# Vision tower on one core: the pre stage of the local attention moved into its loop, keys and values unpadded

## What is computed

```
h = window_attention(x)                        # 8x8 windows, rotary, 8 heads of 8
h = h + local_attention(layernorm(h))          # the part that changes
h = h + routed_ffn(layernorm(h))
h = h + decayed_linear_attention(layernorm(h))
h = h + binary_gated_ffn(layernorm(h))
```

## Time and profile before

| | us |
|---|---|
| median of 3 runs | 1968.52 (1965.01 to 1970.42) |
| the profiled execution | 1966.1 |
| its span, first to last instruction | 1964.3 |
| busy: TensorE, weight loads, VectorE, ScalarE, GpSimd | 1667.3, 1223.0, 1181.7, 975.4, 422.3 |
| mean granted clock of TensorE | 0.959 |

### The profile page before, as it was taken

One profiled execution on the slowest core, in us unless ns is written; L12 is line 12 of the kernel. 1 busy time (PEld: TensorE's weight loads), 2 busy tenths in 40 slices (PEclk: granted clock), 3 DMA queues, 4 the chain that ended last, 5 costly groups with the idle time before them and its releaser, 6 DMA issues.

```text
span 1964.3 us, 94305 instructions
## 1 busy us (share of the span) xinstructions
PE 1667.3 (85%) x35690; PEld 1223.0 (62%) x35690; DVE 1181.7 (60%) x3445; ACT 975.4 (50%) x1765; POOL 422.3 (21%) x477
## 2 busy tenths in 40 slices
PE   5999999856568888888888779999999999999996
PEld 3566666644356666667667556666666666666663
DVE  2466656577534444444444467777777777777772
ACT  2344444423322222222222227777777777777776
POOL 2100000034323232333323222222222222222210
PEclk8899999988889999999999869999999999999998
DMA  4000000135533333333333213333333333333332
GB/s 127 16 11 13 11 11 13 32 64 102 99 94 92 96 92 96 91 96 93 95 96 93 65 29 81 79 80 79 79 80 80 80 80 80 80 80 80 80 79 57
DMA packets 254173, 141.71 MB, mean 72 GB/s; under 512 B 181314, under 2 KB 218050, under 8 KB 253858
## 3 DMA queue, kind: packets, MB, share of 16 engines
q1 hardware_dynamic: 254114, 140.88, 29.8%
HBM read 63.56 MB, written 18.42 MB: 42 GB/s over the span
## 4 chain that ended last, share of the span: by engine, by line
PE 37%; issue 30%; SPq 24%; DVE 5%; DMA 1%; POOL 1%; ACT 1%; DVEq 0%; POOLq 0%; ACTq 0%
SPq L402 12%; PE ps_D L805 11%; DVE prob L1304 4%; SPq L391 3%; PE ps_AV L822 3%; SPq L373 2%; PE ps_J L913 2%; PE ps_J L881 2%; PE ps_J L863 2%; PE ps_OT L891 1%; PE ps_J L939 1%; PE ps_OT L931 1%; PE ps_D L923 1%; PE ps_OT L956 1%; PE ps_OT L875 1%
## 5 line engine op out<-in xcount | busy, mean ns | idle before, releaser
L1062 ACT ACTIVATE prob<-ps_D 128x1024 bf16<-128x1024 f32 x448 | 450.5, 1022 | 80.9 <-PE ps_D L805 80.6
L1234 DVE TENSOR_REDUCE m_sb<-ps_D 128x4 f32<-128x400 f32 x256 | 135.4, 571 | 204.5 <-PE ps_D L708 188.9
L1050 ACT ACTIVATE prob<-ps_D 100x512 f32<-100x512 f32 x256 | 138.8, 594 | 216.9 <-PE ps_D L730 216.9
L493 POOL TENSOR_TENSOR tile_a<-q_st,q_mask 128x1024 f32<-128x1024 f32 x64 | 123.3, 1926 | 404.2 <-DMA q_st<-q_d 346.9
L730 PE MATMUL ps_D<-tile_a,key_patch 64*100 64x128 f32 x2048 | 176.7, 288 | 0.0
L726 PE MATMUL ps_D<-mT,key_rows 64*100 64x128 bf16 x1024 | 129.4, 224 | 50.8 <-ACT mT L1039 32.2
L1187 DVE TENSOR_REDUCE top<-ps_D 128x8 f32<-128x512 f32 x128 | 79.5, 684 | 148.0 <-PE ps_D L582 148.0
L805 PE MATMUL ps_D<-tile_b,w_parts 128*128 128x256 bf16 x1024 | 154.2, 273 | 15.7 <-DVE prob L1304 8.3
L805 PE MATMUL ps_D<-tile_a,w_parts 128*128 128x256 bf16 x1024 | 155.6, 275 | 13.8 <-DVE prob L1304 7.2
L730 PEld LDWEIGHTS ps_D<-tile_a,key_patch 64*100 64x100 f32 x2048 | 146.9, 166 | 0.0
L1304 DVE TENSOR_SCALAR prob<-ps_D 128x1024 bf16<-128x1024 f32 x64 | 78.4, 1225 | 77.9 <-PE ps_D L805 77.9
(11 more groups left out here) (174 smaller groups left out, 3874.9 us busy)
## 6 DMA issues: line engine op xcount, KB each, us to landing
tile_b<-v_d SPq DMA_DIRECT2D x640, 40.0 KB
tile_a<-xg SPq DMA_DIRECT2D x384, 64.0 KB, 2.0
tile_b<-xg SPq DMA_DIRECT2D x384, 64.0 KB, 2.0
key_st<-k_d SPq DMA_DIRECT2D x64, 175.0 KB, 3.0
key_st<-k_d SPq DMA_DIRECT2D x64, 167.0 KB, 3.1
w_exp<-experts SPq DMA_DIRECT2D x64, 129.0 KB, 2.3
k_d<-kpad SPq DMA_DIRECT2D x32, 140.0 KB, 2.3
xin<-in_x SPq DMA_DIRECT2D x32, 128.0 KB, 2.2
```

The costliest lines, as they stand in the source:

```text
L493: gp.tensor_tensor(q_block[:, par, :].rearrange("c (p h q) -> c p h q", h=NH, q=NQ), q_st[:, :].rearrange("c (p a q) -> c p a q", a=1, q=N ...
L1050: act.activation(prob1[0:NKL, 2 * g + x, :], s_loc[x][0:NKL, :], ACT.Exp).then_inc(T2["exp_done"], 1)
L1062: act.activation(sgn[:, k % 4, :], unit(k, par)[:, :], ACT.Sign).then_inc(BN["sign"], 1)
L1234: dve.tensor_reduce(m_sb[:, C * x + HOT[x] + 4 * g:C * x + HOT[x] + 4 * g + 4], m_loc[x][:, 0:4 * NKL].rearrange("p (u n) -> p u n", u=4), ...
```

## The change

Pre and local become one loop over strips of 256 tokens. Each engine's `front` first does the pre work of 5 strips (`LEAD`), then strip i of the loop also does the pre work of strip i+5. On VectorE and GpSimd the moments, 1/std and normalised rows are one strip further ahead (`made`). The order on TensorE within a strip is new: both `peak` halves come right after the `scores` halves, the maxima are transposed ahead of the second `values`. The pre products use free columns of the banks T, OT and J1.

In DRAM the tokens lie unpadded, all images one after the other, with a guard at both ends. Within a row the 64 columns are ordered by column modulo 4 (four groups of 16), so ScalarE writes `xnp` in this order. The ten key columns of the 16 patches are then three groups (4, 3 and 3 columns), each of which is a run of 16 neighbouring tokens, so the values come in three transfers of 4 KB pieces, which ScalarE issues. GpSimd makes `key_patch` with two copies instead of one. Keys outside an image are no longer zeros but what lies there; the edge flags mask them as before. SyncE stores a strip's keys, queries and values in one transfer each. `strips_ahead` writes out two strips ahead of the loop and six behind it.

```diff
-PW = W + 2 * HALF
+NC = W // QP
+GUARD = 16
+EDGES = GUARD + HALF * W
+FLAT = B * H * W + 2 * EDGES
...
-        kpad, q_sb, v_sb = sb("kpad", [C, 2, WIN * PW]), sb("q_sb", [P, 2, 512]), sb("v_sb", [P, 2, 4, C])
+        xn = sb("xn", [P, 2, C])
+        xnp = sb("xnp", [P, 2, 256])
...
         xfgT, xrT = sb("xfgT", [P, 256]), sb("xrT", [P, 256])
         ln_sb = {}
...
+            full = (NSTRIP - LEAD - 1) // 2
+            with eng.Fori(1, full) as j:
                 strip(j, 0)
                 strip(j, 1)
-            strip(NSTRIP // 2 - 1, 0)
...
+                strip(j, 0)
+                strip(j, 1)
+
+        def ahead(j, par):
+
+            i = j * 2 + par
+            m = i + LEAD
+            return m if not isinstance(i, int) or m < NSTRIP else None
+
+        def made(j, par):
+
+            i = j * 2 + par
+            return min(i + LEAD + 1, NSTRIP) if isinstance(i, int) else i + LEAD + 1
...
+        def value_rows(i, group):
+
+            first, n = ((0, QP), (1, 3), (NC - 1, 3))[group]
+            src = v_d[bass.ds(i * (QP * W) + GUARD + first, NC), :]
+            return bass.AP(src.tensor, src.offset, [[W * C, KS], [NC * C, n], [1, NC * C]])
+
+        def value_keys(par, group):
+
+            at, n = ((0, QP), (QP * KS, 3), (7 * KS, 3))[group]
+            return v_patch[at:at + KS * n, par, :, :].rearrange("k a c -> k (a c)")
 
...
+            def store_rows(m, par):
+                at = bass.ds(m * (QP * W) + EDGES, QP * W)
+                sp.wait_ge(L["k_sb"], times(m + 1))
                 settle(sp)
...
+                sp.dma_start(k_d[:, at], kpad[:, par, :]).then_inc(L["stored%d" % par], 16)
+                sp.wait_ge(L["q_sb"], times(m + 1))
                 settle(sp)
...
+                sp.dma_start(q_d[bass.ds(m, 1), :, :].rearrange("t (x c) n -> c (t x) n", c=C),
                              q_sb[C:P, par, :].rearrange("c (a n) -> c a n", n=P)).then_inc(L["stored%d" % par], 16)
-                sp.wait_ge(L["v_sb"], times(i + 1))
+                sp.wait_ge(L["v_sb"], times(m + 1))
...
+                sp.dma_start(v_d[at, :].rearrange("(p t) c -> p (t c)", t=2), v_sb[:, par, :, :].rearrange("p t c -> p (t c)")).then_inc(L["stored%d" % par], 16)
+
+            def stored(pair, par):
+                sp.wait_ge(L["stored%d" % par], times((pair + 1) * 48))
+
+            def keys_in(i):
+                sp.wait_ge(T2["k_patch"], times(i * 2))
                 settle(sp)
                 for x in range(2):
-                    n = KS * PW - 32 * x
...
+                    sp.dma_start(key_st[rows_of(x), :], k_d[:, bass.ds(i * (QP * W) + GUARD - 8 + 8 * x, KS * W + 8)]).then_inc(T2["k_in"], 16)
                 sp.wait_ge(T2["q_block"], times(i))
                 settle(sp)
                 sp.dma_start(q_st[:, :], q_d[bass.ds(i, 1), :, :].rearrange("a r n -> (a r) n")).then_inc(T2["q_in"], 16)
+
+            def edge_in(i, par):
                 sp.wait_ge(T2["scores"], credited((i - 1) * 2))
...
-                sp.dma_start(key_rows[EDGE[0]:C + EDGE[1] + 1, par, :], a["edge"][bass.ds(s, 1), :, :].rearrange("a x n -> (a x) n")).then_inc(T2["edge_in%d" % par], 16)
...
-                    src = v_d[bass.ds(b, 1), bass.ds((s * QP + r) * PW, PW), :].rearrange("a n c -> (a n) c")
-                    sp.dma_start(v_patch[r * KS:(r + 1) * KS, par, :, :], bass.AP(src.tensor, src.offset, [[C, KS], [QP * C, 16], [1, C]])).then_inc(T2["v_in%d" % par], 16)
-
...
-                    strip_in(b, pair * 2, 0)
-                    strip_in(b, pair * 2 + 1, 1)
...
+            def front():
+                store_rows(0, 0)
+                store_rows(1, 1)
+                sp.wait_ge(L["padded"], times(16 * 4))
+                stored(0, 0)
+                stored(0, 1)
+                keys_in(0)
+                store_rows(2, 0)
+
+            def strip(j, par):
+                i = j * 2 + par
+                flat = isinstance(i, int)
+                edge_in(i, par)
+                if not flat or i + 2 < NS:
+                    stored(j + 1, par)
+                if not flat or i + 1 < NS:
+                    keys_in(i + 1)
+                if not flat or i + 3 < NS:
+                    store_rows(i + 3, 1 - par)
+
+            strips_ahead(sp, front, strip)
...
                 v = buf[:, :]
-                return bass.AP(v.tensor, v.offset, [list(v.ap[0]), [QP, 8], [PW, KS], [1, KS]])
+                near = bass.AP(v.tensor, v.offset + 8, [list(v.ap[0]), [1, 8], [NC, QP * KS]])
+                far = bass.AP(v.tensor, v.offset + 9, [list(v.ap[0]), [1, 8], [NC - 2, 2], [W, KS], [NC, 3]])
+                return near, far
...
+            def norm_and_bias(m):
+                inv_std("pre", L, m)
+                bias_rows(m)
+
+            def bias_rows(m):
+                gp.wait_ge(L["xn"], times((m + 1) * 2))
                 settle(gp)
...
+                gp.tensor_tensor(h[:, bass.ds(m * 2, 2), :], h[:, bass.ds(m * 2, 2), :],
+                                 bias2[:, :].rearrange("p (a c) -> p a c", a=1).broadcast_to((P, 2, C)), ALU.add).then_inc(L["biased"], 1)
...
+                keys = key_patch[:, par, :].rearrange("c (p n) -> c p n", p=8)
+                near, far = patches(key_st)
+                gp.tensor_copy(keys[:, :, 0:QP * KS], near).then_inc(T2["k_patch"], 1)
+                gp.tensor_copy(keys[:, :, QP * KS:NKL].rearrange("c p (b r w) -> c p b r w", b=2, r=KS), far).then_inc(T2["k_patch"], 1)
...
+            def front():
+                for m in range(LEAD + 1):
+                    norm_and_bias(m)
+                gp.wait_ge(T1["scores"], times(NT * 2))
+                strip_patches(0, 0)
+                strip_patches(1, 1)
+
+            def strip(j, par):
+                i = j * 2 + par
+                m = made(j, par)
+                nxt = not isinstance(i, int) or i + 2 < NS
+                if not isinstance(m, int) or m < NS:
+                    inv_std("pre", L, m)
+                if nxt:
+                    strip_patches(i + 2, par)
+                if not isinstance(m, int) or m < NS:
+                    bias_rows(m)
+
+            strips_ahead(gp, front, strip)
...
+            def pre_values(m, par):
+                pe.wait_ge(L["xT_sb"], times(m + 1))
+                pe.wait_ge(L["v_sb"], times(m))
                 settle(pe)
-                for t in range(4):
-                    mm = pe.matmul(bank["J2"][:, t * C:(t + 1) * C], xnp[:, par, t * P:(t + 1) * P], w_v2[:, :], start=True, stop=True)
+                for t in range(2):
...
                 mm.then_inc(L["v_ps"], 1)
 
...
+            def pre_keys(m, par, added):
+                pe.wait_ge(L["k_sb"], times(m))
+                pe.wait_ge(L["q_sb"], times(m))
+                pe.wait_ge(T2["h_done"], times(added))
+                settle(pe)
+                pe.matmul(bank["J1"][:, 256:512], w_kq2[:, :], xnp[:, par, :], start=True, stop=True).then_inc(L["kq_ps"], 1)
...
             def strip(j, par):
                 i = j * 2 + par
+                m = ahead(j, par)
                 first, last = isinstance(i, int) and i == 0, isinstance(i, int) and i == NS - 1
                 scores(j, par, 0)
+                if not last:
+                    peak(*after(j, par), 0)
+                if m is not None:
+                    pre_turn(m)
                 if not first:
-                    project(i - 1)
+                    project(i - 1, min(i + LEAD, NS) if isinstance(i, int) else i + LEAD)
+                if m is not None:
+                    pre_values(m, 1 - par)
                 scores(j, par, 1)
                 if not last:
-                    peak(*after(j, par), 0)
+                    peak(*after(j, par), 1)
                 values(j, par, 0)
+                if m is not None:
+                    pre_keys(m, 1 - par, i)
                 if not last:
-                    peak(*after(j, par), 1)
+                    turn_maxima(i + 1, made(j, par))
                 values(j, par, 1)
-                if not last:
-                    turn_maxima(i + 1)
 
             strips_ahead(pe, front, strip)
-            project(NS - 1)
...
+            def pre_turned(m, par):
+                act.wait_ge(L["xT_ps"], times(m + 1))
+                act.wait_ge(L["kq_ps"], times(m - 1))
+                act.activation(xnp[0:C, par, :].rearrange("c (r b q) -> c r b q", r=QP, b=QP),
+                               bank["T"][0:C, 256:512].rearrange("c (r q b) -> c r b q", r=QP, b=QP), ACT.Copy).then_inc(L["xT_sb"], 1)
+
...
+            def values_in(i, par, group):
+                act.wait_ge(T2["av_done"], credited((i - 1) * 2))
+                settle(act)
+                act.dma_start(value_keys(par, group), value_rows(i, group)).then_inc(T2["v_in%d" % par], 16)
 
             def strip(j, par):
                 i = j * 2 + par
-                for g in range(2):
+                m = ahead(j, par)
+                more = not isinstance(i, int) or i + 1 < NS
+
```

(37 more changed lines are left out.)

186 lines of the change are left out of this document (73 added, 113 removed).

## The result

The changed kernel takes 1852.44 us (median of 4 runs, 1851.32 to 1856.05) beside 1966.76 of the kernel before in the same comparison (1961.82 to 1970.42): a ratio of 0.942, 95% interval 0.940 to 0.945, **faster**. The profiled execution took 1851.3 us, 1849.4 of it in the span; 1851.8 had been forecast for it.

A forecast was written before the change was run, and what follows sets the result against it. SyncE's issues were taken to set the 8.80 us strip. First scores at 427.5 plus 576.2 of loop (58 strips at 9.03) end the local stage at 1003.7, not 1118: 114.3 less, 1854 us, range 1840 to 1881 (0.62).

The forecast's parts named there:

- its sum of 5.95 us: SyncE per strip: 8.80 less 5.55 for ten value issues, plus 2.7 for three stores, under the strip's 9.03.
- The front: Pre work of five strips ahead of the loop: 2.8 us a turn, first scores at 427.5, bounds 422 and 436.
- Rival E: Front: six GpSimd power-and-bias pairs and the first stores hold it to 460; +33 us, 1887; chance 0.06.
- TensorE's own work: TensorE in a strip: 7.51 us, the stretch less two waits, kept unchanged, plus 1.32 of pre work.
- The projection's margin: TensorE's cover while VectorE makes the weighted outputs: thin, 0.3 us; 0.20 a strip left for such waits.
- the step on **VectorE: VectorE in a strip: 4.1 us busy plus 1.5 of pre work, 5.6 of 9.03.
- GpSimd's copies: Two strided key_patch copies: 1.1 us a strip, bounds 0.87 and 2.6; margin 1.6 us at 0.87.
- Rival B: GpSimd late with the patches, deciding once copies exceed 2.5 us; at 3.6, +64 us, 1918; chance 0.05.
- rival C: SyncE's store wait joins stores and loads into one ring of 13.1 us a strip; +236 us, 2090; chance 0.02.
- A: Hand-over waits stay at 1.19 us a strip, a fifth piece on every engine pushing others; +57, 1911; chance 0.14.
- F: Moving issues to ScalarE frees nothing, both engines' issues sharing one place; 11.5 us a strip, +143, 1997; chance 0.01.
- D: Loop: all waits gone and added work 1.1, a strip of 8.6 us; 1829; chance 0.10.

The follow-up runs named there:

- experiment 1: Changed kernel, with SyncE instead of ScalarE issuing the three value transfers, in the same strip, not one ahead: 1859.71 us, ratio 0.944.
- experiment 2: Changed kernel, with SyncE issuing the values in ten transfers a strip instead of three by ScalarE: 2139.39 us, ratio 1.086.
- pre apart (3): Changed kernel, with all 64 turns of pre work ahead of the first strip and none in the loop: 2033.16 us, ratio 1.033.
- experiment 4: Changed kernel, with all pre work ahead of the loop and SyncE issuing the queries before the keys: 1942.01 us, ratio 0.985.
- experiment 11: Changed kernel, with the old order of peaks and their transpose on TensorE and of maxima on VectorE: 1890.08 us, ratio 0.961.
- gap and queries first (9): Changed kernel, with the normalise between the two maxima and SyncE loading queries ahead of keys: 1812.74 us, ratio 0.9205.
- experiment 6: Changed kernel, with the key copies into patches moved from GpSimd to ScalarE, as three copies: 1831.01 us, ratio 0.930.
- experiment 7: Changed kernel, with the normalise between the two maxima and GpSimd's next power behind its copies; transfers unchanged: 1853.53 us, ratio 0.937.
- experiment 5: Changed kernel, with VectorE's normalise ahead of the queries' scaling instead of behind it: 1850.08 us, ratio 0.938.
- experiment 8: Changed kernel, with only SyncE's order changed, the queries issued before the keys without waiting for the key copies: 1853.93 us, ratio 0.939.
- experiment 10: Changed kernel, with the normalise between the two maxima, queries issued before keys, and key copies on ScalarE: 1833.14 us, ratio 0.927.

## Why the prediction was right, point by point

**The total** was 2 us off, and that close it is luck: three sizes in the strip were wrong and offset one another to 0.03 us a strip.

**What bounded the kernel** was right. SyncE left the chain, and its sum of 5.95 us held: it waits 3.5 us of 9.0 a strip, 2.9 of them for GpSimd. Experiments 1 and 2 show that the count of value transfers puts it on the path, not who issues them: three from SyncE 9.13 us a strip, ten 13.8. The forecast got the relief from the move to ScalarE; three issues left on SyncE do nearly as well.

**The front** was right: 425.25 for 427.5, with 3.03 us a turn for 2.8, at the half clock as forecast. Its transposes began at 401.48 for 403.5, in the stage ahead, so the front itself took 23.8 us for 24.0. Rival E falls. The first strip and the last five took 1003.1 − 425.25 − 522 = 55.9 us for 52.5.

**TensorE's own work** is where the sum was off. The forecast was 7.51 + 1.32 = 8.83, and 0.20 of waits. Measured: (522 − 41.5) / 58 = 8.28, and 0.72 of waits. The added pre groups are larger than half of the earlier trace rows: in the chain of the kernel after, L733, L741 and L749 hold 3.8 + 6.7 + 7.0 = 17.5% of the time, 1.58 us a strip. So what was 7.51 must now be 6.7. Of the difference 0.15 is a reading: the two rows of waits that I took off (85.8 us) are not all of TensorE's idle time, which is 559 − 463.7 = 95.3 us in the earlier trace rows, so its own time was 7.36. The rest is real and goes with the stops, as a look across the kernels shows (us from one query block on GpSimd to the next, within 0.05 of the stages' figures; own time is the strip less TensorE's waits):

```
kernel, stretch                            strip   waits   own    own less 1.58 of pre work
before, 620:1080                           8.83    1.48    7.35
pre apart (3), 660:1060                    8.80    1.54    7.25
pre apart, queries first (4), 660:1040     7.33    0.36    6.97
old order of the peaks (11), 450:900       9.65    0.96    8.69   7.1
kernel after, 450:940                      9.05    0.72    8.33   6.75
gap and queries first (9), 450:900         8.40    0.15    8.26   6.7
```

Each stop that goes takes more with it than its own row. My step "TensorE's own work is the stretch less its waits", carried over unchanged, was the mis-sized term: −0.8 us a strip, against +0.26 for the pre work and +0.52 for the waits.

Where the time went can be read from the same traces, counted from the end of one group to the end of the next, less the idle time between. From the kernel before to the kernel after the two peaks fall from 1.07 to 0.72 us a strip (0.74 in experiment 4, 0.82 in 11), the transpose of the maxima from 0.33 to 0.11, and the scores from 2.86 to 2.75; the values (2.06) and the projection (1.03 and 1.09) do not fall. The transpose takes 0.33 us, and 0.12 of idle time ahead of it, in every kernel of the table in which it stands right behind values, experiment 4 among them, which has the new order but no pre work in the loop; it takes 0.11 and no idle time where the pre stage's key product runs right ahead of it. So for the transpose it is the pre group that fills what was lost between others. Why the peaks are shorter, 0.35 us, was not tried by itself and stays open.

**The waits** went where it was said for the scores and the peaks (85.8 to 7.7 us; experiment 11 brings part of them back). The projection's margin, called thin at 0.3, did not hold: 0.58 a strip against the 0.20 taken. Its price came from the step on **VectorE**, where I summed 5.6 us of work and let each instruction keep the duration of its row. The normalise does not: 0.31 us with GpSimd at rest, 0.71 beside the copies, 1.07 beside the query block. Experiments 6 and 7 free it in two ways, by moving the copies and by moving it, and 5 moves it from one GpSimd instruction to the next. Experiments 7 to 9 with the kernel after are the four cases of two edits, so they also say what it costs once the ring is out of the way: 9.07 − 8.40 = 0.67 us a strip (8 against 9). VectorE was busy 6.6 us a strip (380.77 / 58). I had looked at the engines' busy shares and not at who runs beside whom. The Trainium skill (SBUF — State Buffer, Who interferes with whom) has a rule that fits: a scaling instruction of VectorE in a mode that uses two ports and a GpSimd instruction take one shared pair of ports, each for its whole length, and the other "fully blocks". Experiment 5 agrees: the first of two normalises, begun 0.43 us behind the start of a block of 1.93 us, ends 0.05 us behind its end. Which mode VectorE ran in no trace here tells.

**ScalarE** was right: its issues take 0.29 to 0.88 us for the 0.8 taken, under the 1.2 at which they would cost. That its room is small was right as well: 1.9 us more of copies (experiments 6 and 10) put it on the path.

**GpSimd's copies** take 0.731 + 1.011 = 1.74 us for 1.1, twice the 0.869 of the earlier trace rows for the same 800 columns in one instruction. The bound of 2.6 held, and the margin too: in the kernel after TensorE's peak never waits for them in 434:956. Rival B falls. (The Trainium skill, GPSIMD Engine Reference, Performance pitfalls for Q7 kernels, would have given an estimated 1.3; the measurement decides, with the split into two instructions in it.) But the ring that the copies belong to I had priced only in the form of rival C. It came out at 9.1 us a strip, as long as TensorE's, and no wait in the kernel after shows it: SyncE waits for GpSimd, GpSimd 217.7 us for the moments, and the chain runs through TensorE. Only taking the other limit away (7) made it visible.

**DMA** stayed hidden, share 0.40, with the queries never awaited (0.5 us, L531).

**The other rivals**: A was nearest, and named the place: TensorE waiting on the projection, VectorE's work. But the waits in all came to 0.72 us a strip for its 1.19, the other hand-over that it called thin, pre's values, never waited, and the cause was the stall, not a fifth piece on every engine. C and F are refuted by SyncE's 2.9 idle us a strip; the move to ScalarE did give little, some 5 to 7 us, but because three issues fit on SyncE as well (experiment 1), not because the issues of both engines go through one place. D's strip of 8.6 comes about in experiment 6, where the projection's wait goes, but with 1.58 us of added work and not D's 1.1.
